# The second attention of a macaron transformer as one run of 64 units, with scores formed twice and the other half's work between them

## The reference

```
x = x + 0.5 * ffn(norm(x));  x = x + attention0(norm(x));  x = x + 0.5 * ffn(norm(x))
x = x + 0.5 * experts(norm(x));  x = x + attention1(norm(x));  x = x + 0.5 * experts(norm(x))
```

```
q, k, v = split(x @ W_qkv.T);  q, k = apply_rope(q), apply_rope(k)
att = where(causal, q @ k.T / sqrt(16), -inf)
y = softmax(att) @ v;  out = y @ W_o.T
```

## Time and profile before

| what | us |
|---|---|
| median of 3 runs | 824.17 |
| the profiled execution | 819.44 |
| its span, first to last instruction | 817.6 |
| busy in the span: PE, DVE, ACT, POOL | 707.6, 618.5, 455.7, 398.2 |
| attention1 from its first matmul to that of the shared expert behind it | 538.40 to 696.15 |

### The profile page before, as it was taken

How to read it: one execution, slowest core, us unless ns; L and a number is a source line. 1 busy time by engine, 2 the same in 40 slices (tenths; PEclk the granted TensorE clock), 3 DMA queues, 4 the chain that set the end, 5 groups by cost and what they waited for, 6 DMA issues and landing times. The chain is left out here.

```text
span 817.6 us, 17561 instructions
## 1 busy us (share of the span) xinstructions
PE 707.6 (87%) x5515; PEld 478.6 (59%) x5515; DVE 618.5 (76%) x1436; ACT 455.7 (56%) x1033; POOL 398.2 (49%) x412
## 2 busy tenths in 40 slices
PE   7899869999979999999898699865897598979994
PEld 3555447777636777755455466433785487645652
DVE  5978877778687777799987677554998597776656
ACT  3544567778757777656423266325574475324551
POOL 4644866666656666447626267434005320341440
PEclk8999989999989999999999899987799599998998
DMA  9999999000000000040001233400000010013324
GB/s 365 333 275 237 130 267 73 0 0 0 1 1 1 0 0 0 1 123 1 1 8 53 81 116 106 148 1 1 1 2 1 14 40 2 2 53 88 116 86 167
DMA packets 64945, 59.07 MB, mean 72 GB/s; under 512 B 29106, under 2 KB 59186, under 8 KB 64370
## 3 DMA queue, kind: packets, MB, share of 16 engines
q1 hardware_dynamic: 60706, 47.85, 25.4%
q0 software_dynamic: 3744, 10.26, 3.5%
q10 hardware_dynamic: 432, 0.15, 0.1%
HBM read 27.92 MB, written 30.33 MB: 71 GB/s over the span
## 5 line engine op out<-in xcount | busy, mean ns | idle before, releaser
L1522 PE MATMUL PS<-XT,WA 128*128 128x512 f16 x432 | 100.2, 380 | 0.0
L616 POOL TENSOR_TENSOR ARENA<-ARENA,ST 128x512 f32<-128x512 f32 x64 | 66.6, 1040 | 64.5 <-DVE ST L1301 64.5
L742 ACT ACTIVATE ARENA<-PS 128x512 f16<-128x512 f32 (+1 forms) x48 | 28.4, 593 | 86.9 <-DVE PS L1179 80.7
L1522 PE MATMUL PS<-WA,ARENA 128*128 128x256 f16 (+2 forms) x960 | 68.3, 212 | 6.0 <-DVE ARENA L1188 4.9
L575 POOL DMA_INDIRECT yt_rows<-WA,DIX x46 | 45.2, 982 | 54.0 <-ACT WA L874 37.1
L1522 PEld LDWEIGHTS PS<-WA,ARENA 128*128 128x128 f16 x960 | 56.7, 97 | 21.9 <-DVE ARENA L1188 10.8
L1522 PEld LDWEIGHTS PS<-XT,WA 128*128 128x128 f16 (+1 forms) x432 | 42.2, 98 | 44.2 <-issue 0.8
L1522 PE MATMUL PS<-KVR,ARENA 128*128 (+1 forms) x384 | 59.0, 283 | 7.9 <-DVE ARENA L1273 5.4
L1281 DVE TENSOR_REDUCE ST<-PS 128x2 f32<-128x512 f32 x64 | 44.0, 687 | 26.4 <-PE PS L1522 25.6
L775 ACT ACTIVATE ARENA<-PS,ST 128x256 f32<-128x256 f32 x128 | 59.3, 470 | 7.8 <-DVE ST L1284 7.6
L1522 PE MATMUL PS<-XT,WC 128*128 128x512 f16 x264 | 60.6, 379 | 2.3 <-DVE T L1170 1.4
(11 more groups left out here) (186 smaller groups left out, 1789.9 us busy)
## 6 DMA issues: line engine op xcount, KB each, us to landing
xs_rows<-ROUT SPq DMA_DIRECT2D x2, 9252.0 KB, 51.2
WA<-xs_rows SPq DMA_DIRECT2D x46, 129.0 KB
WB<-wb_dram SPq DMA_DIRECT2D x1, 4096.0 KB, 21.8
WC<-wc_dram SPq DMA_DIRECT2D x1, 2304.0 KB, 26.9
WA<-wa_dram SPq DMA_DIRECT2D x4, 512.0 KB, 7.8
WA<-wa_dram SPq DMA_DIRECT2D x1, 2048.0 KB, 13.2
WA<-yt_rows SPq DMA_DIRECT2D x4, 512.0 KB, 4.2
WB<-yt_rows SPq DMA_DIRECT2D x4, 512.0 KB, 5.9
```

The lines of the kernel that those rows point to most:

```text
L616: pl.tensor_tensor(pr, pr, rs.broadcast_to([P, 2, S]), ALU.mult).then_inc(norm_done, 1)
L742: sc.activation(HH[r, a, 0, :], hidden_tile(f, hf, j, a), ACT.Copy).then_inc(hid_hi, 1)
L1522: ins = te.matmul(dst, left(a), right(b), start=first and n == 0, stop=last and n == 2, skip_group_check=True)
```

## The change

attention1 becomes one run of 64 units w, written out one behind the other (no loop on the device): `unit(w)` gives the half, the head and the batch of it. For each unit PE forms the scores twice: with the rows as queries, two units ahead, for the maxima (`scores_of`, banks 0 and 1), and with the rows as keys (`turned_scores`, banks 4 and 5). The shift is added to the turned scores, from which two exponentials on ACT make the high part (f16) and the f32 values; POOL subtracts the one from the other for the low part. So the f32 transposes of the exponentials, ACT's copies and DVE's low parts go. The keys are no longer padded: both score matmuls run over the 64 rows `r` of one head, the mask, the shift and the values over 128.

What stood between the halves lies between units, at the numbers w that the constants give: queries and keys, values, turns of queries and of keys of tiles 5 to 7 (each turn with its own copies), the first half's output, its turn and routing. Tile 4's queries, keys and values and the whole of turn(4, 1) go ahead of the first unit. The scatter of the first half's tokens goes beside `glu(3, 0)`. Buffers: six for high and low parts, three for the f32 exponentials. The core of the diff:

```diff
+            return SIDE + 1 if t >= TPH else t % 2
+
+        def q_bank(t):
+            return SIDE + 1 if t >= TPH else SIDE
+
+        K_BANK = SIDE + 1
+        Q_AT, V_AT, TQ_AT, TK_AT = (None, 4, 11, 17), (None, 9, 16, 22), (5, 12, 18, 24), (7, 14, 20, 26)
+        OUT_AT = UN + 5
 
         def up_bank(f, a):
...
                 t = HOSTED[f, hf]
                 if t and j < 2:
                     turn(*t, (j,))
-                if (f, hf) == (2, 0) and j < TPH:
-                    scatter(3, 0, (j,))
+                if f >= 2 and hf == 0 and j < TPH:
+                    scatter(GLU_TURN[f], 0, (j,))
 
             def scatter(n, hf, tiles=range(TPH)):
...
+            def scores_of(w):
+
+                hf, g, i = unit(w)
+                r = slice(g % 2 * P // 2, (g % 2 + 1) * P // 2)
+                after(pe, shift1_done, 2 * (w - 2) + 2)
+                for qt, c0 in ((0, 0), (1, P)):
+                    te.matmul(PS[:, i, c0:c0 + (qt + 1) * P], QT1[hf][r, g // 2, i * S + qt * P:i * S + (qt + 1) * P],
+                              KT1[hf][r, g // 2, i * S:i * S + (qt + 1) * P], start=qt == 0, stop=False,
+                              skip_group_check=True)
+                te.matmul(diagonal(i), IDB[:, :], twice(MASK[:, :]), start=False, stop=True,
+                          skip_group_check=True).then_inc(scores1, 1)
+
+            def turned_scores(w):
+
+                hf, g, i = unit(w)
+                r = slice(g % 2 * P // 2, (g % 2 + 1) * P // 2)
+                bank = keys_bank(w)
+                after(pe, exp1_done, w - 1)
+                for kt in range(2):
+                    te.matmul(PS[:, bank, 2 * kt * P:2 * P + kt * P], KT1[hf][r, g // 2, i * S + kt * P:i * S + (kt + 1) * P],
+                              QT1[hf][r, g // 2, i * S + kt * P:(i + 1) * S], start=kt == 0, stop=False,
+                              skip_group_check=True)
+                te.matmul(diagonal(bank), MASK[:, :], twice(IDB[:, :]), start=False, stop=False, skip_group_check=True)
+
+            def shift(w):
+                hf, g, i = unit(w)
+                bank = keys_bank(w)
+                pe.wait_ge(shift1_done, 2 * w + 2)
+                for qt in range(2):
+                    ins = te.matmul(PS[:, bank, qt * P:(1 + 2 * qt) * P],
+                                    MB1[:, g % 2, 2 * qt + i:2 * qt + i + 1].broadcast_to([P, P]),
+                                    twice(IDB[:, :]) if qt else IDB[:, :], start=False, stop=qt == 1,
+                                    skip_group_check=True)
+                ins.then_inc(shifted1, 1)
+
+            def values_of(w):
+
+                hf, g, i = unit(w)
+                pe.wait_ge(pt1_lo, w + 1)
+                after(pe, o1_done, w // 2 - 1)
+                for qt in range(2):
+                    for kt in range(qt + 1):
+                        blk = qt + kt
+                        c0 = (2 * i + qt) * 32
+                        ins = product(PS[:, value1_bank(g), c0:c0 + VC1], lambda s: PT1[:, w % 6, s, blk * P:(blk + 1) * P],
+                                      lambda s: VB1[:, s, TPH * hf + 2 * i + kt, g, :], kt == 0, kt == qt)
+                ins.then_inc(pv1_done, 1)
```

```diff
+                scores_of(0)
+                scores_of(1)
+                for w in range(2 * UN):
+                    turned_scores(w)
+                    shift(w)
+                    if w == UN - 2:
+                        pe.wait_ge(q1_copied, TT)
+                        pe.wait_ge(k1_copied, TT)
+                    if w + 2 < 2 * UN:
+                        scores_of(w + 2)
+                    if w >= 3:
+                        values_of(w - 3)
+                    if w in Q_AT:
+                        t = TPH + Q_AT.index(w)
+                        pe.wait_ge(rope1_mul, 3 * t)
+                        queries_keys1(t)
+                    if w in V_AT:
+                        t = TPH + V_AT.index(w)
+                        pe.wait_ge(k1_copied, t)
+                        values1(t)
...
+                        turn_k(t)
+                    if w == OUT_AT:
+                        turn(5, 0)
+                    if w in (OUT_AT + 3, OUT_AT + 4):
+                        output(w - OUT_AT - 3)
+                    if w == OUT_AT + 9:
+                        turn(6, 0)
+                    if w == OUT_AT + 12:
+                        route_logits(6, 0)
+                    if w == OUT_AT + 16:
+                        prefix(6, 0)
+                for w in range(2 * UN - 3, 2 * UN):
+                    values_of(w)
+                pe.wait_ge(idx_done, 3)
                 turn(5, 1)
-                output(1)
+                output(2)
+                output(3)
 
```

On the other engines (POOL, ACT, DVE):

```diff
+            def attention1():
+                rotated1(0)
+                rotated1(1)
+                q1_low(0)
+                k1_low(0)
+                q1_low(1)
+                k1_low(1)
+                rotated1(2)
+                turn(4, 1, (0,))
+                rotated1(3)
+                q1_low(2)
+                k1_low(2)
+                turn(4, 1, (1,))
+                q1_low(3)
+                k1_low(3)
+                rotated1(TPH)
+                for w in range(2 * UN):
+                    pool.wait_ge(exp1_done, w + 1)
+                    pl.tensor_tensor(PT1[:, w % 6, 1, :], PR1[:, w % 3, :], PT1[:, w % 6, 0, :],
+                                     ALU.subtract).then_inc(pt1_lo, 1)
+                    if w == 2:
+                        q1_low(TPH)
+                    if w == 3:
+                        k1_low(TPH)
+                    if w - 3 in Q_AT:
+                        rotated1(TPH + Q_AT.index(w - 3))
+                    if w - 5 in Q_AT:
+                        q1_low(TPH + Q_AT.index(w - 5))
+                    if w - 6 in Q_AT:
+                        k1_low(TPH + Q_AT.index(w - 6))
+                    if w == OUT_AT + 6:
+                        turn(6, 0)
```

```diff
+                for w in range(2 * UN):
+                    bank = keys_bank(w)
+                    act.wait_ge(shifted1, w + 1)
+                    after(act, pv1_done, w - 5)
+                    sc.activation(PT1[:, w % 6, 0, :], PS[:, bank, 0:384], ACT.Exp, bias=LNSP[:, :],
+                                  scale=SC1 / SQ ** 2).then_inc(pt1_hi, 1)
+                    after(act, pt1_lo, w - 2)
+                    sc.activation(PR1[:, w % 3, :], PS[:, bank, 0:384], ACT.Exp, bias=LNSP[:, :],
                                   scale=SC1 / SQ ** 2).then_inc(exp1_done, 1)
...
+            def maxima(w):
+                hf, g, i = unit(w)
+                dve.wait_ge(scores1, w + 1)
+                for qt, cols in ((0, slice(0, P)), (1, slice(P, 3 * P))):
+                    v.tensor_reduce(MB1[:, g % 2, 2 * qt + i:2 * qt + i + 1], PS[:, i, cols], AX.X, ALU.max,
+                                    negate=True).then_inc(shift1_done, 1)
```

```diff
+                maxima(0)
+                maxima(1)
+                for w in range(2 * UN):
+                    if w + 2 < 2 * UN:
+                        maxima(w + 2)
+                    if w >= 5 and w % 2:
+                        normalise((w - 5) // 2)
+                    if w - 1 in Q_AT:
+                        rotate1(TPH + Q_AT.index(w - 1))
+                    if w - 1 in V_AT:
+                        values1_low(TPH + V_AT.index(w - 1))
+                    if w - 1 in TK_AT:
+                        keys1(TPH + TK_AT.index(w - 1))
+                    if w == OUT_AT + 1:
+                        turn_low(5, 0)
+                    if w == OUT_AT + 5:
+                        turn_stats(6, 0)
+                    if w == OUT_AT + 7:
+                        turn_norm(6, 0)
+                    if w == OUT_AT + 10:
+                        turn_low(6, 0)
+                    if w == OUT_AT + 13:
+                        routing_ranks(6, 0)
+                    if w == OUT_AT + 18:
+                        routing_slots(6, 0)
+                    if w == OUT_AT + 20:
+                        routing_weights(6, 0)
```

More of the change, by code:

```diff
@@ L57 @@
 NG1 = H1
+UN = 2 * H1
 BLK1 = 3
@@ L668, in _ @@
                     results(0, i - 2)
-                if i in (5, 11, 17):
-                    prepare1(i // 6)
-            prepare1(3)
+            ones1()
             turn(4, 0)
-            for i in range(TPH):
-                rotated1(i, i % 2)
-                qk1_low(i, i % 2)
-            turn(4, 1)
[L677 to L681, removed]
-            scatter(6, 0)
+            attention1()
             run_glu(pool, 3, 0, glu_step, glu_side)
@@ L1817, in scores_of @@
-            def scores_of(hf, p, q):
-                bank = 4 if q % 2 else 2 * hf
-                after(pe, exp1_done, NG1 * hf + 4 * p + q - 1)
-                for i in range(2):
-                    for qt, c0 in ((0, 0), (1, P)):
-                        te.matmul(PS[:, bank + i, c0:c0 + (qt + 1) * P],
```

(34 more changed lines are left out.)

462 lines of the change are left out of this document (167 added, 295 removed).

## The result

The change made the kernel slower: a median of 827.62 us over 14 runs against 822.04 over 14 of before, a ratio of 1.0059 over the compared runs with a 95% interval of 1.0037 to 1.0082 (the quotient of the two medians is 1.0068). The forecast was 816. The time is inside the range, which is as wide as its rivals made it, but the sign is wrong: 0.6% longer where 1% shorter was forecast.

The account below looks back on a forecast made before the run. PE and DVE together bound a step before; PE was to bound the new units. +1.8 before the first shift, −10.5 from there to glu(3,0) and +0.7 for the scatter gave −8.0: 816 us on the median, range 796 to 838.

Parts of the forecast that it names:

- The unit: PE's time per unit in the loop: 1.355 us, of which 0.42 for four changes of matmul height at 0.105 each.
- a free change: Rival: in the units the change between 64 and 128 rows is hidden, unit 0.945, about 797 us; 12%.
- one at 0.2: Rival: at each unit's two score groups every change of height costs 0.2 or more; 845 us at 0.22; 15%.
- The point that was to decide: Shift to shift without side work 1.3 to 1.4 us; outside 1.2 to 1.5 the prediction is wrong, whatever the total.
- The preparation: Stretch before the first shift: +1.8 us, with DVE's two added statistics costing nothing if beside the wait for POOL.
- The bound of +6: Upper bound on the +1.8 before the first shift: both statistics of turn(4,1) in series.
- this start: Low clock at the loop's first shift, once only: 5 us at half speed, loss 2.5, plus 0.5 for the first Exp.
- the two stops: In the loop, DVE's turn_stats (3.43) and routing ranks (4.53) stop the units for 1.3 and 2.4 us.
- The end: Behind the units: turn(5,1) to glu(3,0) stays 6.14 us; the last chain adds 2.87, 2.03 comes off, net +0.84.
- 115.4: Forecast us from first shift to glu(3,0): 86.7 units, 14.7 side work, 4 waits, 3.0 clock, 6.14 and 0.84 end.
- The rival that the clock stays low in the loop: At 1.2 GHz a unit takes at least 2.3 us in the loop: +60, 876 and more; 5%.
- the rival on side work: Side work between units stops them through in-order engines: 12 us more than the 4 for waits, about 828; 15%.

Follow-up runs that it names:

- e5_rows128: The changed kernel with both score matmuls of a unit over all 128 rows (another function); a unit took 0.94 us from shift to shift.
- e2_ranks: The changed kernel with the routing's ranks cut into five pieces on VectorE, one per unit, and prefix, slots and weights three units later; ratio to before 0.9989.
- f4_grouped: The changed kernel with a unit's four 64-row matmuls next to each other, two changes of height per unit instead of four; ratio to before 0.9885.
- e3_prep: The changed kernel with the preparation reordered: rotations of tiles 2 and 3 ahead of turn(4,1)'s statistics, that turn later on the other engines; ratio to before 1.0033.
- p1_prep_narrow: e3_prep with GpSimd's low parts of queries and keys of tiles 2 and 3 for one head instead of sixteen; first shift 30.77 us behind the stage's start.
- h1_stop: e2_ranks with ten extra unused reduces of 512 columns on VectorE in a clean stretch of units; the execution took 845.29 us.

## Why the prediction was wrong

**The unit was right.** 1.355 forecast, 1.34 measured; 0.105 per change of height, 0.10 by e5_rows128. The rivals of a free change and of one at 0.2 fall. The point that was to decide ("outside 1.2 to 1.5") held, and the total was wrong all the same: the argument took the unit for the only large term.

**The preparation was mis-sized**: +1.8 forecast, +7.0 measured; 1.3 of these are not the order's, since the first 24 matmuls took 6.90 instead of 5.56 at a granted clock of 0.58 instead of 0.72, and 5.57 and 5.55 in e2_ranks and f4_grouped. The step that failed is the one on DVE: "nothing, if they lie beside the wait for POOL". The statistics did not lie beside POOL's chain but in it, since POOL's order puts the low part of tile 2 behind a rotation that stands behind a statistic (2 to 3.5, e3_prep); and work beside POOL is not free (3.6 in two statistics, p1_prep_narrow). The bound of +6 named the case and was not taken.

**The clock was taken as a cost of the start alone**: "Afterwards this start occurs once". The start cost 0.8 of its 3.0 (the first four units took 5.46; three of them have no values yet, so 4 x 1.345 − 0.69 = 4.7 were due), but the two stops, foreseen nearly at their length (1.16 and 2.69 for 1.3 and 2.4), each took the clock with them. The first was to cost 1.3: 10.29 for four units and a turn, less 4 x 1.345 and 0.88, is 4.0. The second was to cost 2.4: from 671.51 to 695.72 eleven units take 24.2 instead of 14.8, so 9.4. The end took 11.14 for 9.0. These are 2.7 + 7.0 + 2.1 − 2.2 = 9.6, and by 9.6 the stretch exceeds 115.4; what is left cancels. The rival that the clock stays low in the loop was written for the whole loop and at 5%; it held for its last sixth, behind a stop. That rival's argument against (0.97 with "the same kind of short matmuls") fails: at the low level these units did not bring the clock back in 20 us, as h1_stop shows, while other short ones did, those of f4_grouped. Its size was off too: at 1.2 GHz a unit takes 2.07, not 2.3.

**Smaller terms**: glu(3, 0) 31.39 instead of 30.15, +1.2 for +0.7. POOL and ACT did not bound.

**What came out by luck.** The 827.6 are all but the 828 of the rival on side work, and its mechanism did not come: between the first shift and the last PE waited four times for longer than 0.15 (0.65, 0.21, 1.16 and 2.69), not a dozen times for a microsecond. The row that this rival was given, 574.49 to 577.92, shows PE busy for 3.17 of 3.43 at half the clock and no stop; the stop, 2.45, lies just ahead of it:

```profile
574.63 0.82 PE L1861 MATMUL PS<-MB,IDB 128*128 128x128 bf16 x4 [2.45 <-DVE MB L1386]
```

## What to carry to other kernels

A stop of an engine that runs at a granted clock costs its length and what the clock loses behind it: ask of each new wait whether the work behind it can bring the clock back, and look for an order of that work that does. Work put "beside" another engine's can have a price, here DVE's and POOL's between SBUF tensors: read durations with the neighbour busy, not alone. Executions that start a stage at another clock are compared piece by piece, with the pieces that the edit does not touch taken off. Before forming a product over fewer rows, count the changes of height per step, and put those of one height together.

## What was not expected of the hardware

- A loop with PE busy for 72.3 of 73.3 us held the clock at 1.00 and, behind a stop of 2.7, the same loop stayed at 0.50 for 20 us (in h1_stop 23) with PE busy throughout. With the 64-row matmuls side by side the clock was back 5.6 us behind a stop of 3.55 (f4_grouped).
- DVE's operations between two SBUF tensors and its norms can take 1.7 to 3.4 times as long beside POOL: 1.79 against 3.48 for four sums, 0.43 against 1.02 for a comparison, 0.70 against 2.41 for two norms. The Trainium skill ("SBUF — State Buffer", Who interferes with whom) says that the two engines share a port pair that one holds for a whole instruction; the traces agree in the lengths, and in that the other one can be late as well: in after, POOL's subtraction that starts 0.02 behind a product of DVE (L1136, 0.42) takes 1.17 instead of 0.91.
- 64-row matmuls on different halves of the rows overlap (starts 0.01 apart).
